# Term-by-term query and key products over three open banks, two value chunks moved, query rows issued before two scatters

## The chip, the cores and the metric

The kernel runs on one core of a Trainium2 chip. The metric is the device time of one execution in microseconds (us), median of several runs, lower is better. TensorE is called PE below, VectorE DVE, ScalarE ACT, GpSimd POOL, SyncE SP.

## The reference

A two-layer block works on 16 images of 192 channels by 32 x 32 pixels, in float32:

```
xn = layer_norm(x) * g + b                      # over a whole image
Q, K, V = depthwise3x3(grouped_1x1(xn))         # 8 heads of 24 channels
x  = w_f @ (V @ softmax(K^T Q / alpha)) + b_f + xn
t  = tokens(x)                                  # 1024 tokens of 192 channels per image
h  = ln(t); qkv = h @ W_qkv.T                   # 6 heads of 32
t += (softmax_causal(q k^T / sqrt(32)) v) @ W_proj.T (+ b_proj), twice projected
t += mixture of 4 experts, top 2, hidden 768, gelu, on ln(t)
```

The change touches only the line `qkv = h @ W_qkv.T` and the order of work around it.

## The kernel before

One program for each engine, with an order written out by hand and counting semaphores between them. A loop over 16 images holds the convolution, the channel attention, the token layer norm, the queries, keys and values, and the causal attention of 8 query chunks (`qc`) of 128 tokens by 6 heads. After it the routed experts run block by block. An image takes about 133 us, so the loop takes some 2130 us, and the experts most of the rest.

The change lies in one stretch of each image, about 17 us long, between the last token chunk of the channel attention and the first scores. All engines' orders there:

- PE: `norm_transposes(i, 0)` transposes the normed tokens of chunks 0 to 3 (T); `queries_keys(i, n)` for n = 0, 1, 2 makes three products of 128 rows by 512 tokens, each of five terms (high and low parts of tokens and weights, float32r) in a bank of its own (n % 4); two `values_of_tokens`; then `norm_transposes(i, 1)`, products 3 to 5, and six value chunks; then `query_scores`.
- PE waits in `queries_keys` on `y_sb`, which counts the token chunks that DVE has taken out of PSUM (`channel_mixed`, L1045). Chunk k of the tokens stands in bank k % 6, so chunk 6 is in bank 0 and chunk 7 in bank 1, and those are banks of products 0 and 1. The wait is `y_sb >= 7` for n = 0 and `y_sb >= 8` for n = 1 to 3.
- DVE, in this order: `channel_mixed` of chunks 5 and 6 with their statistics, `low_channels(i, 0)` (the low parts of T, L1029 and L1032), `channel_mixed` of chunk 7, `low_qk(i, 0)` (the low part of product 0, L1038), `normed(i, 1)` (the normed tokens of chunks 4 to 7, L1021 and a copy), `low_qk` of products 1 and 2, `low_channels(i, 1)`, `low_qk` of products 3 to 5.
- ACT: `high_channels(i, 0)` (L1458), products 0 to 2 out of PSUM (L1551), values 0 and 1 (L1462), `high_channels(i, 1)`, products 3 to 5, values 2 to 7.
- POOL: `token_rstd` (L716), `send` (L780, indirect DMAs that scatter the normed rows of the image before, two for each chunk), the query rows of wave 0 (`load_queries`, L357, six DMAs, after three products are out), more `send`, `output_bias(i, 0)` (L786), `inverse_wide` (L728, L729) for each query chunk, on which PE's `norms` waits.
- SP: key rows of wave 0 (`load_keys`, L351), then wave 1 and 2 of keys and queries. `query_scores(i, 0)` waits for `qk_lo` of all six products and for wave 0.

Of the kernel before, what the change touches and what calls it, by code (L numbers as in the profile page):

```python
# [15 lines left out]
P = 128  # L16
# [3 lines left out]
def hybrid_block_kernel(nc, x, ln_g, ln_b, conv_w, conv_bias_row, conv_taps, conv_bias, alpha_rows, w_f_t, b_f,  # L20
# [4 lines left out]
    NC = N // P  # L25
# [45 lines left out]
    with ExitStack() as ctx:  # L71
# [387 lines left out]
        def value_bank(k):  # L459
            return (6, 7, 4, 5)[k % 4]  # L460
# [189 lines left out]
        def _(pool):  # L650
# [138 lines left out]
            for i in range(B):  # L789
# [7 lines left out]
                if i:  # L797
                    send(i - 1, 5, 6)
# [7 lines left out]
                if i:  # L806
                    send(i - 1, 6, NC)
# [615 lines left out]
        def _(act):  # L1423
# [102 lines left out]
            for i in range(B):  # L1526
# [15 lines left out]
                for n in range(NQ):  # L1542
                    if n == QK_FIRST:
                        for k in range(2):
                            values_out(i, k)
                        high_channels(i, 1)
                    f, nh = QK_ORDER[n]
                    if i == 0 and n == 0:
                        act.wait_ge(w_ld["zero"], 16)
                    act.wait_ge(qk_ps, NQ * i + n + 1)  # L1550
                    a.activation(QKh[:, f, BANK * nh:BANK * (nh + 1)], bank(n % 4), ACT.Copy).then_inc(qk_hi, 1)  # L1551
                for k in range(2, NC):
                    values_out(i, k)
# [55 lines left out]
        def _(pe):  # L1609
# [110 lines left out]
            def queries_keys(i, n):  # L1720
                f, nh = QK_ORDER[n]
                if n >= 4:
                    pe.wait_ge(qk_lo, NQ * i + n - 3)
                if n < 4:
                    pe.wait_ge(y_sb, NC * i + min(NC - 1 + n, NC))
                for m, (act_part, w_part) in enumerate(qkv):
                    if f == 0 and m in (0, 3):
                        pe.wait_ge(T_hi, 4 * i + 2 * nh + 1 + m // 3)
                    if f == 0 and m in (2, 3):
                        pe.wait_ge(T_lo, 4 * i + 2 * nh + m - 1)  # L1730
                    last = t.matmul(bank(n % 4), w_part[:, P * f:P * (f + 1)],
                                    act_part[:, BANK * nh:BANK * (nh + 1)], start=m == 0, stop=m == 4)
                last.then_inc(qk_ps, 1)

            def values_of_tokens(i, k):
                if k >= 4:
# [110 lines left out]
            for i in range(B):  # L1847
# [35 lines left out]
                for n in range(QK_FIRST):  # L1883
                    queries_keys(i, n)
# [3 lines left out]
                for n in range(QK_FIRST, NQ):  # L1888
                    queries_keys(i, n)
                for k in range(2, NC):  # L1890
# [182 lines left out]
```

## Time and profile before

| | us |
|---|---|
| median of 3 runs | 3336.41 (3331.54 to 3340.59) |
| the profiled execution | 3334.18 |
| its span, first to last instruction | 3332.3 |
| PE busy | 3067.4 (92%) |
| DVE busy | 2202.3 (66%) |
| ACT busy | 1871.5 (56%) |
| POOL busy | 874.5 (26%) |
| mean granted PE clock | 0.984 |

A row of the timeline is an instruction (or some alike, `xN`): its start, its duration, engine, line, output and inputs, and in brackets how long the engine had been idle and what released it. PE's instructions overlap, so durations of neighbours add up to more than the distance of their starts: for PE the starts are the thing to subtract.

### The profile page before, as it was taken

How to read it: one execution, taken by the hardware profiler on the slowest of the kernel's cores; microseconds unless marked ns; L12 is line 12 of the kernel's file. 1: busy time of each engine (PE TensorE's matmuls, PEld its weight loads, DVE VectorE, ACT ScalarE, POOL GpSimd, SP SyncE). 2: the span in 40 equal slices, each digit the busy share in tenths (PEclk: the TensorE clock that was granted, in tenths of full speed). 3: DMA queues.
4: the chain of work that ended last, by engine and by line, in shares of the span. 5: the costliest groups of instructions: out<-in, count | busy, mean ns of one | idle time of the engine just before them, and what ended most of it. 6: DMA issues, size and time to landing. Idle time of an engine off the chain costs nothing. (4 is left out here: it accounts for less than half of the span.)

```text
span 3332.3 us, 72396 instructions
## 1 busy us (share of the span) xinstructions
PE 3067.4 (92%) x26642; PEld 2344.2 (70%) x26642; DVE 2202.3 (66%) x5619; ACT 1871.5 (56%) x3996; POOL 874.5 (26%) x1142
## 2 busy tenths in 40 slices
PE   4999999999999999999999999958999999999995
PEld 1666667666666676666766766637888888888884
DVE  3777677677776776777767767664555655655653
ACT  0647456465474664654746647535555555555553
POOL 2121313303223133132230331450223223223222
PEclk9999999999999999999999999979999999999997
DMA  7546445454364454544644546515667767667673
GB/s 177 142 114 178 115 124 148 124 150 126 113 184 116 122 149 122 153 118 120 173 125 115 148 123 154 156 47 159 195 206 213 221 208 220 210 205 228 206 212 120
DMA packets 256516, 519.82 MB, mean 156 GB/s; under 512 B 70919, under 2 KB 161991, under 8 KB 246521
## 3 DMA queue, kind: packets, MB, share of 16 engines
q1 hardware_dynamic: 222878, 453.58, 48.6%
q0 software_dynamic: 29184, 59.81, 6.0%
q8 instruction: 217, 3.56, 0.4%
q10 hardware_dynamic: 4107, 1.81, 0.3%
q14 instruction: 130, 1.06, 0.1%
HBM read 242.82 MB, written 117.71 MB: 108 GB/s over the span
## 5 line engine op out<-in xcount | busy, mean ns | idle before, releaser
L1051 DVE TENSOR_REDUCE minus_max<-ps 128x1 f32<-128x128 f32 (+7 forms) x768 | 571.6, 750 | 243.7 <-PE ps L1772 232.3
L1469 ACT ACTIVATE p_sb<-ps,minus_max 128x128 f32<-128x128 f32 (+7 forms) x768 | 569.3, 741 | 41.3 <-DVE minus_max L1051 37.8
L1782 PE MATMUL ps<-ident,p_sb 128*128 128x128 f32 x3456 | 530.6, 279 | 44.2 <-ACT p_sb L1469 18.4
L1356 DVE TENSOR_TENSOR g_lo<-g,g_hi 128x512 fp32r<-128x512 f32 x402 | 282.8, 704 | 369.3 <-ACT g_hi L1593 369.3
L1592 ACT ACTIVATE g<-ps,bcur 128x512 f32<-128x512 f32 x402 | 276.6, 688 | 429.2 <-PE ps L1967 429.2
L1483 ACT ACTIVATE PT<-ps 128x512 f32<-128x512 f32 (+3 forms) x768 | 396.7, 517 | 132.7 <-PE ps L1782 123.5
L1782 PEld LDWEIGHTS ps<-ident,p_sb 128*128 128x128 f32 x3456 | 370.0, 141 | 99.4 <-ACT p_sb L1469 37.5
L1983 PE MATMUL ps<-w_all,g_hi 128*128 x1608 | 434.6, 351 | 0.0
L1770 PE MATMUL ps<-KS,QS 96*128 96x512 f32 (+3 forms) x1152 | 393.6, 401 | 21.4 <-ACT p_sb L1469 17.9
L1647 PE MATMUL ps<-ring,wconv 125*32 125x512 f32 (+1 forms) x3072 | 358.4, 606 | 15.0 <-DMA ring<-padded_scratch 15.0
L780 POOL DMA_INDIRECT routed_rows<-xhat,slot x256 | 253.3, 989 | 358.2 <-issue 358.2
L846 POOL DMA_INDIRECT got<-expert_rows,slot x256 | 257.6, 1006 | 333.6 <-issue 270.7
L728 POOL COPY inverse_wide<-inverse_sums 128x192 f32<-128x192 f32 x128 | 44.2, 345 | 1040.3 <-DVE inverse_sums L1072 1040.3
L1988 PE MATMUL ps<-w_all,g_lo 128*128 x1608 | 293.1, 264 | 0.0
L1988 PEld LDWEIGHTS ps<-w_all,g_lo 128*128 128x128 f32 x1608 | 289.4, 188 | 2.0
L1983 PEld LDWEIGHTS ps<-w_all,g_hi 128*128 128x128 f32 x1608 | 263.8, 191 | 22.8
L1593 ACT ACTIVATE g_hi<-ps,bcur 128x512 fp32r<-128x512 f32 x402 | 273.5, 680 | 0.0
L1967 PE MATMUL ps<-X_hi,cur 128*128 128x512 f32 x804 | 264.9, 411 | 7.5 <-ACT g_hi L1593 5.6
L1967 PE MATMUL ps<-X,cur 128*128 128x512 f32 x804 | 250.0, 392 | 0.0
L1770 PEld LDWEIGHTS ps<-KS,QS 96*128 96x128 f32 x1152 | 196.9, 195 | 69.4 <-ACT p_sb L1469 42.4
L1647 PEld LDWEIGHTS ps<-ring,wconv 125*32 125x32 f32 (+1 forms) x3072 | 94.2, 111 | 207.5 <-issue 192.7
L1064 DVE COPY PT<-ps 128x128 f32<-128x128 f32 (+3 forms) x384 | 184.9, 482 | 67.6 <-PE ps L1782 67.5
(276 smaller groups left out, 5442.5 us busy)
## 6 DMA issues: line engine op xcount, KB each, us to landing
ring<-padded_scratch SPq DMA_DIRECT2D x576, 204.0 KB
cur<-w_all SPq DMA_DIRECT2D x67, 1536.0 KB, 7.1
routed_rows<-zero_rows SPq DMA_DIRECT2D x67, 384.0 KB, 5.0
xgt<-routed_rows SPq DMA_DIRECT2D x67, 384.0 KB, 4.6
expert_rows<-y_rows SPq DMA_DIRECT2D x67, 384.0 KB, 3.0
padded_scratch<-xpad SPq DMA_DIRECT2D x32, 435.0 KB, 3.6
x_sb<-x SPq DMA_DIRECT2D x16, 768.0 KB, 5.5
KS<-QKh SPq DMA_DIRECT2D x128, 96.0 KB
```

The source lines that it names most:

```text
L1051: v.tensor_reduce(nmx[:, qc, h:h + 1], score_place(n), AX, ALU.max, negate=True).then_inc(mx_sb, 1)
L1356: v.tensor_tensor(g_lo[:, n % 2, :], g32[:, n % 2, :], g_hi[:, n % 2, :].bitcast(F32), ALU.subtract).then_inc(lo_sb, 1)
L1469: a.activation(p_sb[n % NP][:, 0:P * (qc + 1)], score_place(n), ACT.Exp, bias=nmx[:, qc, h:h + 1], accum_out=ls[:, qc, h:h + 1]).then_inc( ...
L1483: a.activation(PT[h][:, k0:k0 + nb, :], bank(pass_bank(t))[:, 0:P * nb].rearrange("p (k q) -> p k q", q=P), ACT.Copy).then_inc(PT_act, 1)
L1592: a.activation(g32[:, n % 2, :], bank(n % 2), ACT.Gelu, bias=b1)
L1593: a.activation(g_hi[:, n % 2, :], bank(n % 2), ACT.Gelu, bias=b1).then_inc(gelu_sb, 1)
L1647: last = t.matmul(bank(2 * (r % 2) + nh)[W * j:W * (j + 1), :], wconv[s][0:KROWS[s], h, c0:c0 + W], rhs, start=s == 0, stop=s == 1, skip_g ...
L1770: t.matmul(o[:, k0:k0 + keys], QS[0:96, qc // TPC, h, P * (qc % TPC):P * (qc % TPC + 1)], KS[0:96, h, k0:k0 + keys], start=True, stop=k0 + ...
L1782: last = t.transpose(bank(pass_bank(piece))[:, P * k:P * (k + 1)], p_sb[n % NP][:, P * (k0 + k):P * (k0 + k + 1)], ident[:, :])
L1967: last = t.matmul(bank(n % 2), w[:, W1L * part + P * j:W1L * part + P * (j + 1)], act_part[:, :], start=m == 0, stop=m == 4)
L1983: t.matmul(bank(acc_bank(r, tt))[:, 0:2 * C], g_hi[:, n % 2, P * tt:P * (tt + 1)], w2j, start=j == 0, stop=False, skip_group_check=True)
L1988: last = t.matmul(bank(acc_bank(r, tt))[:, 0:C], g_lo[:, n % 2, P * tt:P * (tt + 1)], w2j[:, 0:C], start=False, stop=j == J - 1, skip_grou ...
```

## The change

Four things change. `queries_keys` takes a half instead of one product: it issues the first two terms of the three products one product after the other, then the third term of all three, then the last two terms. The banks stay the same and so do the waits, but they now stand ahead of the groups of terms. Value chunks 2 and 3 move from behind products 3 to 5 to in front of them, right behind the second transposes, on PE and in ACT's order. The value chunks get other banks (6, 7, 6, 7, 4, 5, 6, 7), with waits for `v_done` to match. On POOL `send(i - 1, 5, 6)`, two scatters, moves from in front of the query rows of wave 0 to behind them.

```diff
--- before.py
+++ after.py
@@ -457,7 +457,7 @@
         NORM_BANK = (6, 4)
 
         def value_bank(k):
-            return (6, 7, 4, 5)[k % 4]
+            return (6, 7, 6, 7, 4, 5, 6, 7)[k]
 
         QK_ORDER = [(0, 0), (1, 0), (2, 0), (0, 1), (1, 1), (2, 1)]
         NQ = len(QK_ORDER)
@@ -794,8 +794,6 @@
                 if i:
                     send(i - 1, 3, 5)
                 token_rstd(i, 1)
-                if i:
-                    send(i - 1, 5, 6)
                 pool.wait_ge(qk_hi, NQ * i + PAIR_GROUPS)
                 for j in range(2):
                     load_queries(g, 0, j, 0, QKh)
@@ -804,7 +802,7 @@
                 for j in range(2):
                     load_queries(g, 0, j, 1, QKl)
                 if i:
-                    send(i - 1, 6, NC)
+                    send(i - 1, 5, NC)
                 output_bias(i, 0)
                 for qc in range(NC):
                     inverse_wide(i, qc)
@@ -1544,12 +1542,14 @@
                         for k in range(2):
                             values_out(i, k)
                         high_channels(i, 1)
+                        for k in range(2, TPC):
+                            values_out(i, k)
                     f, nh = QK_ORDER[n]
                     if i == 0 and n == 0:
                         act.wait_ge(w_ld["zero"], 16)
                     act.wait_ge(qk_ps, NQ * i + n + 1)
                     a.activation(QKh[:, f, BANK * nh:BANK * (nh + 1)], bank(n % 4), ACT.Copy).then_inc(qk_hi, 1)
-                for k in range(2, NC):
+                for k in range(TPC, NC):
                     values_out(i, k)
                 for n, (qc, h) in enumerate(SOFT):
                     exponentials(i, n)
@@ -1717,23 +1717,36 @@
 
             qkv = ((T0, wqa_hi), (T0, wqa_lo), (T2, wqa_hi), (T1, wqb_hi), (T1, wqb_lo))
 
-            def queries_keys(i, n):
-                f, nh = QK_ORDER[n]
-                if n >= 4:
-                    pe.wait_ge(qk_lo, NQ * i + n - 3)
-                if n < 4:
-                    pe.wait_ge(y_sb, NC * i + min(NC - 1 + n, NC))
-                for m, (act_part, w_part) in enumerate(qkv):
-                    if f == 0 and m in (0, 3):
-                        pe.wait_ge(T_hi, 4 * i + 2 * nh + 1 + m // 3)
-                    if f == 0 and m in (2, 3):
-                        pe.wait_ge(T_lo, 4 * i + 2 * nh + m - 1)
-                    last = t.matmul(bank(n % 4), w_part[:, P * f:P * (f + 1)],
+            def queries_keys(i, nh):
+                group = range(QK_FIRST * nh, QK_FIRST * (nh + 1))
+
+                def term(n, m):
+                    f = QK_ORDER[n][0]
+                    act_part, w_part = qkv[m]
+                    return t.matmul(bank(n % 4), w_part[:, P * f:P * (f + 1)],
                                     act_part[:, BANK * nh:BANK * (nh + 1)], start=m == 0, stop=m == 4)
-                last.then_inc(qk_ps, 1)
+
+                pe.wait_ge(T_hi, 4 * i + 2 * nh + 1)
+                for n in group:
+                    if n >= 4:
+                        pe.wait_ge(qk_lo, NQ * i + n - 3)
+                    else:
+                        pe.wait_ge(y_sb, NC * i + min(NC - 1 + n, NC))
+                    term(n, 0)
+                    term(n, 1)
+                pe.wait_ge(T_lo, 4 * i + 2 * nh + 1)
+                for n in group:
+                    term(n, 2)
+                pe.wait_ge(T_hi, 4 * i + 2 * nh + 2)
+                pe.wait_ge(T_lo, 4 * i + 2 * nh + 2)
+                for n in group:
+                    term(n, 3)
+                    term(n, 4).then_inc(qk_ps, 1)
 
             def values_of_tokens(i, k):
-                if k >= 4:
+                if k in (2, 3):
+                    pe.wait_ge(v_done, NC * i + k - 1)
+                if k in (6, 7):
                     pe.wait_ge(v_done, NC * i + k - 3)
                 for m, (act_part, w_part) in enumerate(qkv):
                     last = t.matmul(bank(value_bank(k))[:, 0:C], act_part[:, P * k:P * (k + 1)],
@@ -1880,14 +1893,14 @@
                     input_and_first_heads(i, k)
                     last_heads(i, k)
                 norm_transposes(i, 0)
-                for n in range(QK_FIRST):
-                    queries_keys(i, n)
+                queries_keys(i, 0)
                 for k in range(2):
                     values_of_tokens(i, k)
                 norm_transposes(i, 1)
-                for n in range(QK_FIRST, NQ):
-                    queries_keys(i, n)
-                for k in range(2, NC):
+                for k in range(2, TPC):
+                    values_of_tokens(i, k)
+                queries_keys(i, 1)
+                for k in range(TPC, NC):
                     values_of_tokens(i, k)
                 if not i:
                     pe.wait_ge(setup_pool, 8)
```

## Rows read from the trace of the kernel before

**Rows 1.** Page, part 1: engine busy us (share of span) xinstructions.

```profile
PE 3067.4 (92%) x26642; PEld 2344.2 (70%) x26642; DVE 2202.3 (66%) x5619; ACT 1871.5 (56%) x3996; POOL 874.5 (26%) x1142
```

**Rows 2.** Timeline, TensorE, first half: start us, us, engine, line, tile, [idle <-releaser].

```profile
775.73 1.09 PE L1714 MATMUL ps<-ident,xhat 128*128 128x128 f32 x8 [0.66 <-DVE xhat L1021]
777.16 0.47 PE L1731 MATMUL ps<-T_hi,wqkv_a_hi 128*128 128x512 f32 x1 [0.34 <-DVE t_sb L1045]
777.47 0.40 PE L1731 MATMUL ps<-T_hi,wqkv_a_lo 128*128 128x512 f32 x1
778.24 0.50 PE L1731 MATMUL ps<-T_lo,wqkv_a_hi 128*128 128x512 f32 x1 [0.37 <-DVE T_lo L1029]
779.05 0.47 PE L1731 MATMUL ps<-T,wqkv_b_hi 128*128 128x512 f32 x1 [0.31 <-DVE T L1032]
779.37 0.39 PE L1731 MATMUL ps<-T,wqkv_b_lo 128*128 128x512 f32 x1
...
781.86 0.25 PE L1739 MATMUL ps<-wqkv_a_hi,T_hi 128*128 128x192 f32 x1
...
782.95 1.04 PE L1714 MATMUL ps<-ident,xhat 128*128 128x128 f32 x8
```

**Rows 3.** Timeline, VectorE, the same image.

```profile
776.70 0.36 DVE L1045 TENSOR_TENSOR t_sb<-ps,bf_bc 128x196 f32<-128x196 f32 x1
...
778.94 0.36 DVE L1045 TENSOR_TENSOR t_sb<-ps,bf_bc 128x196 f32<-128x196 f32 x1
...
780.42 0.69 DVE L1038 TENSOR_TENSOR QKl<-ps,QKh 128x512 fp32r<-128x512 f32 x1 [0.30 <-ACT QKh L1551]
781.28 1.35 DVE L1021 TENSOR_SCALAR xhat<-t_sb,tmv,rstd 128x192 f32<-128x192 f32 x4 [0.17 <-POOL rstd L716]
...
782.87 1.28 DVE L1038 TENSOR_TENSOR QKl<-ps,QKh 128x512 fp32r<-128x512 f32 x2
784.22 0.69 DVE L1029 TENSOR_TENSOR T_lo<-ps,T_hi 128x512 fp32r<-128x512 f32 x1
```

**Rows 4.** Timeline, ScalarE, the same image.

```profile
779.79 0.60 ACT L1551 ACTIVATE QKh<-ps 128x512 fp32r<-128x512 f32 x1 [2.29 <-PE ps L1731]
```

**Rows 5.** Timeline, TensorE, second half of the same image.

```profile
784.33 0.47 PE L1731 MATMUL ps<-T_hi,wqkv_a_hi 128*128 128x512 f32 x1 [0.34 <-ACT T_hi L1458]
...
788.62 0.25 PE L1739 MATMUL ps<-wqkv_a_hi,T_hi 128*128 128x192 f32 x1
...
791.96 0.24 PE L1770 MATMUL ps<-KS,QS 96*128 96x128 f32 x1
```

**Rows 6.** Timeline, GpSimd, the same image; last row: the next image.

```profile
783.84 2.29 POOL L357 DMA_DIRECT2D QS<-QKh  x4
...
791.34 0.96 POOL L780 DMA_INDIRECT routed_rows<-xhat,slot  x1 [1.50 <-issue]
...
793.58 1.87 POOL L786 TENSOR_TENSOR t_sb<-t_sb,bproj_bc 128x784 f32<-128x784 f32 x1
797.45 0.34 POOL L728 COPY inverse_wide<-inverse_sums 128x192 f32<-128x192 f32 x1 [2.00 <-DVE inverse_sums L1072]
...
930.74 0.34 POOL L728 COPY inverse_wide<-inverse_sums 128x192 f32<-128x192 f32 x1 [3.28 <-DVE inverse_sums L1072]
```

**Rows 7.** Timeline, DMA issues of SyncE's queue, same image.

```profile
782.68 2.57 SPq L351 DMA_DIRECT2D KS<-QKh  x4
```

**Rows 8.** DMA issues of 782 to 793 us: out<-in, count, KB, us to landing.

```profile
QS<-QKl POOLq DMA_DIRECT2D x2, 96.0 KB, 4.7
```

**Rows 9.** Groups by line, whole span: count | busy, mean ns | idle, releaser.

```profile
L1731 PE MATMUL ps<-T,wqkv_b_hi 128*128 128x512 f32 x96 | 40.4, 420 | 9.8 <-DVE T L1032 9.8
```

**Rows 10.** Timeline, TensorE, first image.

```profile
105.42 1.09 PE L1714 MATMUL ps<-ident,xhat 128*128 128x128 f32 x8 [1.60 <-DVE xhat L1021]
```

**Rows 11.** Windows, TensorE: us, busy (x), granted clock, DMA share, GB/s.

```profile
107.00:110.00 3.00, 2.94 (x6) 0.50 0.00 0
```

**Rows 12.** Timeline, TensorE, third image, attention part.

```profile
323.48 0.41 PE L1814 MATMUL ps<-PT,v_sb 128*32 128x128 f32 x4 [2.23 <-issue]
```

## The prediction

> **What bounds the kernel now.** I read the page first: PE is busy 92% of the span, more than any other engine [rows 1], so a change pays only where it takes idle time from PE. Then the groups by line, for the lines that the change touches. There the idle time is small and evenly spread: the last wait of each half, for DVE's low part of T1, is 9.8 us over 32 halves, 0.31 us each [rows 9]. Then the timelines of one image in the middle of the loop, from the first transposes at 775.73 to the first score at 791.96, 16.23 us [rows 2 to 5]. The reader is to see four waits ahead of the terms of product 0: 0.34 (high part of T0, and token chunk 6), 0.37 (low part of T0), 0.31 (low part of T1) [rows 2], and 1.38 us from the start of the second transposes to product 3, of which 0.34 or so is idle [rows 2, 5]. With about as much again in the second half the waits come to some 1.65 us an image, 26 us over 16 images. That is what the change could take at most.
>
> **Pitches.** All from starts. 512-column terms: eleven from 779.37 to 781.86, 0.2265 us each; the first after a wait 0.31 (777.16 to 777.47) [rows 2]. Value terms: 30 from 788.62 to 791.96, 0.111 each [rows 5]. A product is taken by ACT 0.42 us after its last term starts (779.37 to 779.79) and takes 0.60 [rows 2, 4]. DVE takes the low part 0.03 after that and each takes 0.69, or 0.64 in a row (1.28 for two) [rows 3].
>
> **Part 1, first half: terms across three banks.** It adds and removes no instruction; 15 terms stay 15 terms. But the waits for `y_sb` stand ahead of each product's first term. Product 1 goes into bank 1, which held token chunk 7, so term (1, 0) waits for `y_sb` 8, and that is DVE's L1045 at 778.94, done at 779.30 [rows 3]: DVE takes chunk 7 out only behind the low parts of T. Before, product 1 began at 779.6, and this wait was hidden behind the five terms of product 0. Now it is the third thing that PE does. So PE issues (0, 0) and (0, 1) at 777.16 and 777.47, and stands from 777.7 to about 779.40 (0.10 us behind 779.30, as 777.16 stands 0.10 behind the chunk taken at 776.70 for 0.36) [rows 2, 3]. Behind it 13 terms are left where before ten were left at 779.6: the last three products end their issue at 779.40 + 0.31 + 12 x 0.2265 = 782.43, against 781.86 before: **0.57 later**. The three waits of 1.02 us in all are replaced by one of about 1.5 us.
>
> **Part 1, who waits for that.** The order of completion changes too. Product 0 was complete with the term at 779.37; now its last term is the ninth of the 13 and starts at 779.40 + 0.31 + 7 x 0.2265 = 781.30. ACT takes it at 781.72 instead of 779.79, DVE's `low_qk(i, 0)` starts at 782.35 instead of 780.42 [rows 3, 4]. Queued behind it on DVE is `normed(i, 1)`: the normed rows start at 782.35 + 0.64 = 782.99 instead of 781.28, take 1.35, and are done at 784.34 [rows 3]. PE's second transposes wait for them. PE is done with values 0 and 1 at 782.43 + 1.10 = 783.53, so there is a new wait of about 0.85 us, and the transposes start at 784.40 instead of 782.95: **1.45 later**.
>
> **Part 2, values 2 and 3 behind the second transposes.** The transposes hold PE 1.0 us, to 785.4. Ten value terms (1.1 us) then fill the time in which ACT and DVE split T: to 786.5. The high part of T0 frees product 3 at 784.40 + 1.38 = 785.8 by the old distance [rows 2, 5], hidden. DVE's low parts start at 782.99 + 1.59 + 1.28 + 0.07 = 785.93 (old distances) and end at 786.6 and 787.3 [rows 3]; term 2 starts at 786.5 + 6 x 0.2265 = 787.9 and term 3 at 788.5, both hidden. So the second half runs without a wait: 15 terms to 789.90, and four value chunks, 20 x 0.111, to **792.12**, against 791.96. The part wins back 1.3 of the 1.45 us. The banks cost nothing: chunks 2 and 3 wait for values 0 and 1 to be out, by 784.1, and PE is there at 785.4. If the cover by values 2 and 3 were not there, the old 1.38 us would stand and the score would be 1.1 later.
>
> **What is late next.** The first score also waits for the low part of product 5. Its last term starts at 786.5 + 14 x 0.2265 = 789.67, so ACT has it by 790.2 to 790.8, behind products 3 and 4, and DVE, which is now in a row of three, ends at 791.8. That is 0.3 us ahead of 792.12: hidden, with little over. So the stretch costs **+0.16 us an image, 2.6 us in 16**.
>
> **Part 3, two scatters moved behind the query rows.** POOL issued the first query row at 783.84, straight behind the scatters, while SP issued its first key row at 782.68 on the same signal [rows 6, 7]. Now product 2 is out at 783.3 (last term 782.20, +0.42, ACT still busy until 782.7, +0.60), so both queues start at 783.3: POOL 0.5 earlier, SP 0.6 later. Wave 0 of the queries, six issues of 0.57 us (2.29 for four), was issued by 787.3, the last one begun at 786.7 and landed up to 4.7 us later [rows 6, 8], so by about 791.4, and the score came at 791.96 with no wait [rows 5]. The low rows of product 2 are there at 785.86; with them the last query row begins at 786.5 and the last key row of wave 0 (0.64 us each, [rows 7]) at 786.7, and 4.7 us more make 791.4, before 792.1. Value of the earlier queries: nothing, nobody waited for them. SP's later waves run 0.6 later as well; their first users stand twelve and more units on, and I give them no price. The price is behind: POOL issues two more scatters, 1.27 us each (0.97 and 0.30 between), ahead of `output_bias(i, 0)` and so ahead of `inverse_wide(i, 0)`, for which PE's `norms` waits. POOL had 2.00 us of room there in this image and 3.28 in the next; the difference is a gap of 1.50 us ahead of the third scatter [rows 6]. Six of 15 images have such a gap. With 2 x 1.27 us more, 0.17 earlier and PE 0.16 later, the room is 1.1 us in nine images and -0.2 in six. Below, the cost is nothing, if the gap goes because two fewer scatters are outstanding ahead of the query rows; above, it is a second gap of 1.50 us in each image: 9 x 0.4 + 6 x 1.7 = 14 us. I take 0 to 1 us, the nearest row being a gap that falls once in six scatters.
>
> **Part 4, the clock.** The new wait of 1.5 us has a neighbour of 0.34 just before it. In the first image PE stood 1.60 us ahead of the transposes [rows 10], then waited 0.34 as everywhere, and from 107 to 110 the granted clock is 0.50, 1.2 GHz instead of 2.4 [rows 11]. Of the idle times under 2 us it is the only one in the loop that was followed by a fall. In that stretch 3 us give the work of 1.5. The other images stand 0.66 us at most here [rows 2] and keep the full clock. In the new order 1.5 + 0.34 us lie within 2.6 us, almost what the first image had. The bounds are no fall (0) and one in each of 15 images (15 x 1.5 = 22 us). More matmul work lies beside the new wait than beside the old one, two 512-column terms, so I take one fall, 1.5 us. The Trainium skill (TensorE: Matmul & The Clock Gate, Why this matters for your kernels) warns against idle gaps between bursts of matmuls, but only of gaps longer than this one; by it no image would lose its clock and the sum would be 1.5 us less. The first image of this trace speaks for the shorter gap.
>
> **The sum.** 3334.18 (profiled) + 2.6 + 0.7 + 1.5 = 3339.0. The profiled execution is 2.2 us below the median of the runs shown, so in their terms **3341.2 us, +0.14%**. About 0.3% (10 us) is what a measurement of this kernel can tell from no change.
>
> **The rivals.** (a) *Slower, by the clock.* The mechanism of part 4 in most images: the wait for chunk 7 lets the granted clock fall just when 13 terms are to be issued. It decides from the fifth image on (2.6 + 5 x 1.5 = 10). For it: the first image. Against it: the busier neighbourhood, and gaps in the attention part, one of 2.23 us, that cost no clock [rows 12]. With eight of 16 falls: 3336.4 + 2.6 + 12 = 3351; with 15, 3361. Chance 0.15. (b) *Slower, by POOL.* A second gap in each image makes `norms` of chunk 0 late: 3336.4 + 2.6 + 14 = 3353. For it: the gaps grow with traffic, and the two scatters now fall among the key and query waves. Against it: nine of 15 images show none. Chance 0.09. (c) *Faster, the change does what it says.* The waits go as intended, if chunk 7 is out by the time PE asks for it: 3336.4 - 26 = 3310; halfway, with the first half as before and only the second half's 0.65 to 1.3 us saved, 3336.4 - 16 x 1.0 = 3320. Against it: DVE's order is untouched, and chunk 7 stands behind both low parts [rows 3]. Chance 0.06. (d) *Forecast*, 3334 to 3346: the wait for chunk 7 eats what values 2 and 3 bring. Chance 0.68. The 0.02 left is a late landing of the key rows, slower.
>
> **How the numbers follow.** Faster 0.06, within 0.3% 0.68, slower 0.26. The range leaves out the faster cases and the worst of (a) and (b): low 3333 (the forecast less the 4.9 us by which the lowest run lies under the median, and the 3 us that I may have the stretch too dear), high 3357.
>
> **What would show it.** In the new trace, per image: PE idle of about 1.5 us ahead of the third 512-column term, released by DVE t_sb L1045; the second transposes about 8.7 us behind the first instead of 7.2, released by DVE xhat; no wait inside products 3 to 5; the first score 16.4 us behind the first transposes. ACT's first product out about 6 us behind the first transposes instead of 4.1. POOL's first query row about 7.6 us behind them, and its wait ahead of the first `inverse_wide` near 1 us or gone. The granted clock at 1.00 in this stretch but for one or two images. I am wrong if the first stand is shorter than 0.5 us, if the transposes wait for something else, if the score waits for key or query rows or the low part of product 5, or if several images show 0.50.

## The result: 3360 us, slower, and the profile after

| | before | after |
|---|---|---|
| median of six runs each, us | 3336.36 (3331.54 to 3340.59) | 3360.14 (3358.64 to 3364.27) |
| profiled execution, us | 3334.18 | 3359.25 |
| its span, us | 3332.3 | 3356.4 |
| mean granted clock | 0.984 | 0.976 |

The ratio is 1.0073, 95% interval 1.006 to 1.0086: 24 us slower. The forecast was 3341.2, the range ended at 3357. That it would be slower had been given 0.26.

The page of the changed kernel, part 1, beside [rows 1]: PE is busy 4.0 us more with the same 26642 instructions, so 20 of the 24 us are idle time of PE.

```profile
PE 3071.4 (92%) x26642; PEld 2356.8 (70%) x26642; DVE 2194.5 (65%) x5619; ACT 1862.6 (55%) x3996; POOL 873.3 (26%) x1142
```

Groups by line (count | busy, mean ns | idle before, releaser). First the transposes' row of the kernel before; its waits for the low part of T1 are in [rows 9]. Then the changed kernel.

```profile
L1714 PE MATMUL ps<-ident,xhat 128*128 128x128 f32 x256 | 34.2, 277 | 10.9 <-DVE xhat L1021 10.9
```
```profile
L1714 PE MATMUL ps<-ident,xhat 128*128 128x128 f32 x256 | 36.4, 287 | 27.2 <-DVE xhat L1019 27.1
...
L1726 PE MATMUL ps<-T_hi,wqkv_a_hi 128*128 128x512 f32 x96 | 45.3, 471 | 26.4 <-DVE t_sb L1043 26.4
L1726 PE MATMUL ps<-T,wqkv_b_hi 128*128 128x512 f32 x96 | 40.3, 420 | 0.0
...
L1835 PE MATMUL ps<-ident,inverse_wide 128*128 128x128 f32 x256 | 56.7, 304 | 15.7 <-POOL inverse_wide L729 15.6
```

**One image in which nothing else is disturbed**, the same as in [rows 2 to 5] (image 5, TensorE; columns as in [rows 2]):

```profile
784.90 1.09 PE L1714 MATMUL ps<-ident,xhat 128*128 128x128 f32 x8 [0.77 <-DVE xhat L1019]
786.38 0.47 PE L1726 MATMUL ps<-T_hi,wqkv_a_hi 128*128 128x512 f32 x1 [0.39 <-DVE t_sb L1043]
786.68 0.40 PE L1726 MATMUL ps<-T_hi,wqkv_a_lo 128*128 128x512 f32 x1
788.52 0.50 PE L1726 MATMUL ps<-T_hi,wqkv_a_hi 128*128 128x512 f32 x1 [1.45 <-DVE t_sb L1043]
...
793.41 1.09 PE L1714 MATMUL ps<-ident,xhat 128*128 128x128 f32 x8 [0.57 <-DVE xhat L1019]
...
801.09 0.25 PE L1783 MATMUL ps<-KS,QS 96*128 96x128 f32 x1
```

This is what was forecast: a stand of 1.45 us for `y_sb` 8, the second transposes 8.51 us behind the first (before: 7.22), then no wait. The score comes 16.19 us behind the first transposes, against 16.23. So in an undisturbed image the new order costs nothing, and the loss is elsewhere.

**The next image** (image 6, TensorE), and the windows of its stretch (us, busy, granted clock, DMA share, GB/s):

```profile
919.64 1.09 PE L1714 MATMUL ps<-ident,xhat 128*128 128x128 f32 x8 [2.10 <-DVE xhat L1019]
921.12 0.65 PE L1726 MATMUL ps<-T_hi,wqkv_a_hi 128*128 128x512 f32 x1 [0.39 <-DVE t_sb L1043]
923.26 0.79 PE L1726 MATMUL ps<-T_hi,wqkv_a_hi 128*128 128x512 f32 x1 [1.07 <-DVE t_sb L1043]
```
```profile
916.00:921.00 5.00, 2.63 (x20) 1.00 0.17 59
921.00:924.00 3.00, 1.81 (x4) 0.54 0.10 34
924.00:928.00 4.00, 4.00 (x11) 0.50 0.16 52
```

Two things are new. PE stands 2.10 us ahead of the *first* transposes, where it stood 0.60 to 0.66 in images 1 to 15 before; and then the granted clock falls to 0.50 (1.2 GHz). The idle time ahead of the first transposes in images 1 to 15 is now 0.60, 0.76, 2.09, 1.56, 0.77, 2.10, 1.20, 1.98, 0.82, 0.76, 1.62, 0.90, 1.55, 0.75, 0.61. In this stretch the clock falls in exactly the seven of them with 1.20 or more (images 3, 4, 6, 7, 8, 11, 13), besides image 0. In five of the seven it is at 0.50 before the stand for `y_sb` 8 begins (from 0.2 us ahead of the first transposes to 2.0 us behind them); in images 7 and 13, with 1.20 and 1.55 us, only when the stand is over, 4.0 us behind them. Image 13, whose first transposes start at 1866.12:

```profile
1861.00:1870.00 9.00, 5.62 (x37) 1.00 0.16 55
1870.30:1873.30 3.00, 3.00 (x8) 0.50 0.20 68
```

**Who releases the first transposes.** VectorE's normed rows, and these wait for POOL's token `rstd` (VectorE, image 6, changed kernel, then the kernel before):

```profile
918.11 1.47 DVE L1019 TENSOR_SCALAR xhat<-t_sb,tmv,rstd 128x192 f32<-128x192 f32 x4 [2.06 <-POOL rstd L716]
```
```profile
907.46 1.47 DVE L1021 TENSOR_SCALAR xhat<-t_sb,tmv,rstd 128x192 f32<-128x192 f32 x4 [0.58 <-POOL rstd L716]
```

And POOL is late because of the first six scatters that stand ahead of it in its queue. GpSimd, image 6, in the kernel before:

```profile
895.69 1.07 POOL L780 DMA_INDIRECT routed_rows<-xhat,slot  x1 [15.72 <-issue]
...
898.33 0.96 POOL L780 DMA_INDIRECT routed_rows<-xhat,slot  x1 [0.30 <-issue]
902.12 0.95 POOL L780 DMA_INDIRECT routed_rows<-xhat,slot  x1 [2.84 <-issue]
...
906.31 1.04 POOL L716 TENSOR_TENSOR rstd<-rstd,minus_half 128x4 f32<-128x4 f32 x1 [0.69 <-DVE rstd L1012]
```

and in the changed kernel:

```profile
904.97 1.07 POOL L780 DMA_INDIRECT routed_rows<-xhat,slot  x1 [15.83 <-issue]
910.90 0.96 POOL L780 DMA_INDIRECT routed_rows<-xhat,slot  x1 [4.87 <-issue]
...
915.96 0.97 POOL L780 DMA_INDIRECT routed_rows<-xhat,slot  x1 [0.30 <-issue]
916.96 1.04 POOL L716 TENSOR_TENSOR rstd<-rstd,minus_half 128x4 f32<-128x4 f32 x1
```

Before, POOL issued three scatters, stood 2.84 us, issued three more and then still waited 0.69 us for VectorE. Now it issues one, stands 4.87 us, and has five scatters of 1.27 us ahead of the `rstd`: the row shows no idle time ahead of it, so VectorE waits for POOL. The gap stood behind the third scatter in each of images 2 to 15 before (1.9 to 2.8 us), and behind the first in each of them now (1.9 to 4.9 us). In both orders that is the seventh scatter counted from the query rows. The changed kernel has a second gap in each of these images, of 1.95 us, behind the fourteenth, between the first and the second `rstd`.

**Where the 24 us lie.** Sums over images 1 to 15 of the profiled executions, from the starts. From the start of PE's last matmuls ahead of the transposes (the row of L1705, `last_heads`) to the first transposes: 16.6 us before, 25.5 after, **+8.9**. From the first transposes to the first score: 244.2 and 254.0, **+9.8**, all of it in six of the seven images with a fall (17.8 to 18.1 us, against 16.2). In the seventh, image 3, the clock is low around the transposes and back when the stand ends; it takes 16.35 us. The first score of image 0 is **+2.6** later, 1.1 of it in image 0's own stretch, with its longer fall. The parts between a score and the next image's L1705 take 0.8 us less in sum. Together these are the 20.5 us by which the last image's first score is later (2130.12 and 2150.66); the last 4 us come behind it.

### The profile page after: what moved, and what is told of

Read it like the earlier page. It is cut to its first block and busy times, and to the rows that moved or that the text cites. A ratio compares the mean times of both kernels' runs of the same rounds, so it can differ in the third digit from the quotient of the medians.

```text
span 3356.4 us, 72396 instructions
## 1 busy us (share of the span) xinstructions
PE 3071.4 (92%) x26642; PEld 2356.8 (70%) x26642; DVE 2194.5 (65%) x5619; ACT 1862.6 (55%) x3996; POOL 873.3 (26%) x1142
## 5 line engine op out<-in xcount | busy, mean ns | idle before, releaser
L1795 PE MATMUL ps<-ident,p_sb 128*128 128x128 f32 x3456 | 532.0, 279 | 44.6 <-ACT p_sb L1467 18.1
```

The costliest lines, as they stand in the source:

```text
L1795: last = t.transpose(bank(pass_bank(piece))[:, P * k:P * (k + 1)], p_sb[n % NP][:, P * (k0 + k):P * (k0 + k + 1)], ident[:, :])
```

## Experiments

Interval and ratio are always against the kernel before on the same chip; its median was 3336 to 3337 us in each comparison.

### The terms and values without the scatters

```diff
 # of the changed kernel
+                if i:
+                    send(i - 1, 5, 6)
                 pool.wait_ge(qk_hi, NQ * i + PAIR_GROUPS)
 ...
-                    send(i - 1, 5, NC)
+                    send(i - 1, 6, NC)
```

> The changed kernel with the two scatters back ahead of the query rows; terms by product group and values 2 and 3 early stay. Theory Q (POOL's queue): the loss comes from the scatters' new place, by the token rstd of the next image that is queued behind them. Then this kernel is 3334 to 3340 us (ratio 0.999 to 1.001), PE's idle time ahead of the first transposes is 0.6 to 0.7 us in all images but the first, and the clock keeps full speed in this stretch in all but the first image or two. Theory C (clock): the 1.45 us wait for token chunk 7 lets the clock fall by itself. Then six or so images show 0.50 and this kernel is 3346 to 3350 us (ratio 1.003 to 1.004).

Measured: 3344.79 us (3339.92 to 3351.56), ratio 1.0025 (1.0014 to 1.0037). The time lies between what the two theories gave. The idle time ahead of the first transposes is back to 0.61 to 0.66 us in every image from 1 on; the 1.45 us stand is there as before, the stretch is 16.48 us, and in this stretch the clock falls in three images (6, 7 and 14, 17.4 us each) and longer in image 0 (18.6). In the three it is at 0.50 from 4.4 us behind the first transposes, just behind the stand. Parts 1, 2 and 4 cost 8.4 us; the forecast had 4.1 for them. 15 of the 24 us come with the scatters.

### The scatters without the terms and values

```diff
 # of the kernel before
-                if i:
-                    send(i - 1, 5, 6)
 ...
-                    send(i - 1, 6, NC)
+                    send(i - 1, 5, NC)
```

> The kernel before with only the two scatters moved behind the query rows. Theory Q: the token rstd comes late and PE idles 0.7 to 2.1 us ahead of the first transposes, some 9 us over the images, and the clock falls in few images or none, as no second long wait follows: 3344 to 3348 us (ratio 1.0025 to 1.0035). If the scatters alone also let the clock fall in six or so images: 3352 to 3356. Theory C: as before, 3334 to 3338.

Measured: 3359.18 us (3353.2 to 3366.54), ratio 1.0067 (1.0052 to 1.0081). My expectation was far too low: two of an image's 16 scatters, moved by some 4 us in the queue, give nearly the whole loss alone. GpSimd, image 6, of this kernel:

```profile
902.71 1.07 POOL L780 DMA_INDIRECT routed_rows<-xhat,slot  x1 [15.85 <-issue]
908.04 0.96 POOL L780 DMA_INDIRECT routed_rows<-xhat,slot  x1 [4.27 <-issue]
...
914.09 1.04 POOL L716 TENSOR_TENSOR rstd<-rstd,minus_half 128x4 f32<-128x4 f32 x1
...
916.67 0.96 POOL L780 DMA_INDIRECT routed_rows<-xhat,slot  x1 [0.30 <-issue]
919.58 0.96 POOL L780 DMA_INDIRECT routed_rows<-xhat,slot  x1 [1.96 <-issue]
...
921.83 1.04 POOL L716 TENSOR_TENSOR rstd<-rstd,minus_half 128x4 f32<-128x4 f32 x1
```

The picture of the changed kernel, without its terms. A second gap of 1.96 us makes the second `rstd` come straight behind the scatters too, so the second transposes are 0.19 us later (7.45 behind the first). The sums: +9.2 us ahead of the first transposes, +8.1 in the stretches (some 4 from the 0.3 us that most are longer, some 4 from the falls in images 3 and 8), 2.7 ahead of the first score of image 0, 1.3 in the attention parts. A further 7.0 us come behind the last image's first score, where the changed kernel has 3.6; their cause is open. The clock falls in three images only (in image 11 it costs nothing), though seven have 1.24 us or more ahead of the transposes: images 6, 7, 13 and 14, with 1.50, 1.24, 1.99 and 1.62, keep it. So does image 0, with 1.61 us, where every other kernel with such an idle time there loses it.

### The stand filled with work

```diff
 # of the changed kernel, ahead of term (1, 0)
+                     if n == 0:
+                         for _ in range(5):
+                             t.matmul(bank(3), wqa_hi[:, 0:P], T0[:, 0:BANK], start=True, stop=True)
```

The five matmuls write a bank that the next product overwrites; they add nothing to the result.

> The changed kernel with five more 512-column matmuls (1.1 us, into bank 3, whose result nobody reads) issued in the wait for token chunk 7. No wait is taken away. Theory: the falls of the clock come from PE standing idle, not from the late data. Then the clock falls vanish from this stretch or become one or two, each image's stretch is 16.2 us, and what is left over before is the 9 us ahead of the first transposes: 3346 to 3350 us (ratio 1.003 to 1.004). If the clock doesn't answer to it: 3358 to 3362.

Measured: 3349.78 us (3344.19 to 3361.16), ratio 1.0046 (1.003 to 1.0062). The stand shrinks from 1.45 to 0.29 us, the first transposes still wait 0.6 to 2.1 us, and the clock falls in image 0 and five later images (3, 6, 8, 10, 14) instead of seven, for 0.6 to 1.0 us each instead of 1.5 to 1.9. The five have 1.65 to 2.09 us ahead of the transposes, but images 5, 7 and 12, with 2.01, 1.57 and 1.65, keep the clock. Image 5, whose first transposes start at 776.56:

```profile
771.00:776.50 5.50, 3.56 (x26) 1.00 0.16 55
776.50:781.00 4.50, 3.76 (x19) 1.00 0.15 54
```

The time overstates what the work in the stand brought. The sums say 6.6 us in the stretches, all of it clock, and 1.9 lost ahead of the first transposes; 6.2 us more lie in attention parts, where the changed kernel has two images that take 5.0 and 1.7 us longer than the usual 116 and this one has none, and 3.0 ahead of the first score. In the first of the two, image 1, the granted clock is 0.50 in two places (262.5 and 327.5 us), the second right behind an idle time of 2.23 us. The kernel before has such longer attention parts too (four, 1.2 to 2.6 us each), with gaps as in [rows 12]; they come and go with the program, and what sets them is open. What the run shows all the same: all its falls in images 1 to 15 begin within 1.9 us of the first transposes, ahead of the place of the stand, so these do not need the stand; none begins behind that place, as two do in the changed kernel.

### Token chunk 7 taken out ahead of the low parts

```diff
 # of the first experiment's kernel, VectorE: channel_mixed(i, 7) now stands ahead of this
-                low_channels(i, 0)
 ...
+                low_channels(i, 0)
```

> As terms_values, and DVE takes token chunk 7 out ahead of the low parts of T instead of behind them. Theory: the wait for chunk 7 cancels what the terms across three banks bring. Then it goes from 1.45 us to under 0.2, the low parts come 0.4 later and stay hidden behind the first two terms of three products or cost 0.2, and the stretch falls from 16.2 to 15.0 to 15.4 us: 3318 to 3326 us (ratio 0.995 to 0.997). If the second half (normed rows behind token rstd and low part of product 0) sets the pace instead, the stretch stays at 16 and the time at 3334 to 3338.

Measured: 3318.62 us (3314.88 to 3320.84), ratio 0.9943 (0.993 to 0.9956). The 1.45 us stand is gone. TensorE, image 5; behind the second row no further wait until the second transposes:

```profile
774.58 1.09 PE L1716 MATMUL ps<-ident,xhat 128*128 128x128 f32 x8 [0.67 <-DVE xhat L1021]
776.05 0.47 PE L1728 MATMUL ps<-T_hi,wqkv_a_hi 128*128 128x512 f32 x1 [0.39 <-DVE t_sb L1045]
781.89 1.09 PE L1716 MATMUL ps<-ident,xhat 128*128 128x128 f32 x8 [0.80 <-DVE xhat L1021]
```

The stretch takes 14.8 to 15.1 us in images 2 to 15. The releaser of the stand is shown: with chunk 7 early, the new order is worth 18 us; with chunk 7 late, it loses 8.

### The terms alone, the values alone

```diff
 # terms_only: of the change, only queries_keys and its two calls
 # values_only: of the change, only these and the banks and waits that go with them
                 norm_transposes(i, 1)
+                for k in range(2, TPC):
+                    values_of_tokens(i, k)
 ...
-                for k in range(2, NC):
+                for k in range(TPC, NC):
```

> The kernel before with only the terms issued product group by product group (values and scatters as before). Theory: the wait for token chunk 7 costs and nothing fills the time behind the second transposes. Second transposes 8.8 us behind the first instead of 7.26, the wait of 1.38 us behind them stays, score at 17.0 us instead of 16.26: 11 us, and 3 us for falls of the clock in some three images: 3347 to 3352 us (ratio 1.003 to 1.005). Rival: the order of terms is neutral, 3334 to 3338.

> The kernel before with only value chunks 2 and 3 behind the second transposes. Theory: it takes the 1.2 us of waits of the second half and has no price: second transposes at 7.26 us, first score at 15.0 us, 3314 to 3320 us (ratio 0.994 to 0.995). Rival: the query rows of wave 0, issued as late as before, land behind the values and PE waits for them: stretch 15.5 to 16, 3324 to 3334.

Measured: the terms alone 3353.63 us (3345.78 to 3361.12), ratio 1.0052 (1.0034 to 1.0069), the second transposes 8.78 us behind the first with 0.81 us idle, stretch 17.0 us, and 17.8 to 18.4 in six images with a fall (3, 5, 7, 9, 11, 14). These six have the usual 0.61 to 0.66 us ahead of the first transposes, and the clock is at 0.50 from 3.7 to 4.7 us behind them: here the stand for chunk 7 brings falls about with nothing else changed. Image 9, where the stand ends at 1322.11:

```profile
1318.40:1322.50 4.10, 2.19 (x12) 1.00 0.23 80
1322.50:1325.50 3.00, 3.00 (x9) 0.50 0.07 22
```

The values alone 3318.68 us (3316.15 to 3330.37), ratio 0.9948 (0.993 to 0.9967), stretch 15.1 us. The sums over images 1 to 15 against the kernel before: +17.9 (some 7 of it from the falls) and -16.3 us. The two halves of the balance that made the forecast have the sign it gave them: the terms make the second transposes 1.5 us late, and values 2 and 3 behind the second transposes are worth 1.1 us an image. But half of the 1.5, 0.8 us, comes back in the second half from the order of terms itself, 0.4 of it since that half waits 0.25 us instead of 0.34 and 0.32. The values alone have the waits of [rows 2] and none in the second half.

### The rstd a scatter group earlier

```diff
 # of the changed kernel
-                    send(i - 1, 0, 3)
+                    send(i - 1, 0, 2)
 ...
-                    send(i - 1, 3, 5)
+                    send(i - 1, 2, 5)
```

> The changed kernel whole, but with four scatters instead of six ahead of the first token rstd, and six instead of four ahead of the second. All scatters stay, and as many stay behind the query rows. Theory Q: the only harm of the scatters' new place is that the first token rstd stands behind a gap that now comes early, so with two fewer ahead of it PE's idle time ahead of the first transposes is 0.6 us again in every image but the first; the second rstd comes later but in time, since the normed rows wait for the low part of product 0 anyway. Stretch 16.2 to 16.5, falls of the clock in three images or so: 3338 to 3346 us (ratio 1.001 to 1.003). Rival (traffic of the later scatters or POOL's lateness at the inverse sums does the harm): 3356 to 3362.

Measured: 3371.23 us (3364.38 to 3379.86), ratio 1.0103 (1.0084 to 1.0123). The first half is as expected: the idle time ahead of the first transposes is 0.60 to 0.66 us again in images 1 to 15, so it is the scatters ahead of the `rstd` that hold it. The total missed, by 25 us and more: six instead of four scatters, with the second gap among them, now stand between the first and the second `rstd`. GpSimd, image 8, and VectorE and TensorE behind it:

```profile
1195.78 0.97 POOL L780 DMA_INDIRECT routed_rows<-xhat,slot  x1 [0.30 <-issue]
1198.71 0.96 POOL L780 DMA_INDIRECT routed_rows<-xhat,slot  x1 [1.96 <-issue]
...
1200.96 1.04 POOL L716 TENSOR_TENSOR rstd<-rstd,minus_half 128x4 f32<-128x4 f32 x1
```
```profile
1202.04 1.26 DVE L1019 TENSOR_SCALAR xhat<-t_sb,tmv,rstd 128x192 f32<-128x192 f32 x4 [1.37 <-POOL rstd L716]
```
```profile
1203.36 1.97 PE L1714 MATMUL ps<-ident,xhat 128*128 128x128 f32 x8 [2.04 <-DVE xhat L1019]
```

The second transposes come 10.0 us behind the first, the stretch takes 17.7 us and up to 20.3 with a fall. In this order the second `rstd` waits behind the scatters instead of the first.

### Two scatters the other way

```diff
 # of the kernel before
-                    send(i - 1, 5, 6)
+                    send(i - 1, 5, 7)
 ...
-                    send(i - 1, 6, NC)
+                    send(i - 1, 7, NC)
```

> The kernel before, but the scatters of token chunk 6 of the image before are also issued ahead of the query rows, and only those of chunk 7 behind them (two scatters, against four in the kernel before and six in the changed one). Theory P (GpSimd's issue gap sits ahead of the eighth scatter counted from the query rows: after three of the next image in the kernel before, after one in the changed one): here the gap comes after five scatters of the next image, so one scatter instead of five or three is left behind it ahead of the token rstd, which is then early or as in the kernel before: idle ahead of the first transposes 0.60 to 0.66 us in all images, no further falls of the clock, 3334 to 3341 us. Theory R (the gap is tied to a time behind the first scatter, about 6 us, not to a count): the gap comes after four scatters and the rstd is no later either; the two are told apart by the place of the gap. Rival S: the query rows, 2.5 us later behind two more scatters, make the first scores late: then more than 3345 us, with the score idle on POOL's queue.

Measured: 3400.75 us (3398.38 to 3401.06), ratio 1.0198 (1.0181 to 1.0215). Two of the three theories were right, each on its own point. GpSimd, image 5:

```profile
777.93 1.07 POOL L780 DMA_INDIRECT routed_rows<-xhat,slot  x1 [15.94 <-issue]
...
783.10 0.96 POOL L780 DMA_INDIRECT routed_rows<-xhat,slot  x1 [0.30 <-issue]
786.00 0.97 POOL L780 DMA_INDIRECT routed_rows<-xhat,slot  x1 [1.94 <-issue]
788.38 1.04 POOL L716 TENSOR_TENSOR rstd<-rstd,minus_half 128x4 f32<-128x4 f32 x1 [1.41 <-DVE rstd L1012]
...
801.18 0.97 POOL L780 DMA_INDIRECT routed_rows<-xhat,slot  x1 [2.01 <-issue]
...
803.42 2.28 POOL L357 DMA_DIRECT2D QS<-QKh  x4
```

The gap stands behind the fifth scatter, in each of images 2 to 15. Over three orders it is so at four scatters behind the query rows and three ahead of the gap, six and one, two and five: **behind the seventh scatter counted from the query rows**. The second gap, at 801.18 here, and those of the changed kernel, `scatters_only` and `rstd_sooner` stand behind the fourteenth. In the kernel before, the fifteenth comes 2.3 us behind the fourteenth in any case, because an `rstd` that waits for VectorE stands between them (image 6), so no gap is seen there. And the first `rstd` has 1.41 us to spare. But a second gap now falls ahead of the query rows, and these are late (TensorE, the first score of the same image):

```profile
809.66 0.30 PE L1770 MATMUL ps<-KS,QS 96*128 96x128 f32 x1 [2.22 <-DMA QS<-QKl]
```

36.7 us of such idle time in all. Query rows that are issued 4.25 us later (12.36 us behind the first transposes, against 8.11 by [rows 2, 6]) make the stretch 2.4 us longer (18.6): they had some 1.9 us of room. The stretches account for 33.9 us and the attention parts for another 24.2: the granted clock goes to 0.50 in each of images 1 to 14 between 0.5 us ahead of the late score and 2.7 us behind it, as from 811 to 820 us in image 5.

### The changed kernel with chunk 7 early

> The changed kernel with all its scatters as it has them, but VectorE takes token chunk 7 out ahead of the low parts of T, so that the wait of 1.45 us for it goes. Theory P (two separate causes: the late token rstd gives 0.6 to 2.1 us of idle ahead of the first transposes, and the clock falls only where that idle and the 1.45 us stand close together): the idle of 0.6 to 2.1 us stays in about seven images, some 10 us in all above the order with the scatters ahead (3318.6 us), and the clock falls in no more than two images besides the first: 3326 to 3332 us. Rival: the idle ahead of the transposes alone lets the clock fall, in about seven images: 3338 us or more.

(The edit is that of `chunk7_early`, with the scatters as the change has them.) Measured: 3331.08 us (3325.66 to 3334.24), ratio 0.9985 (0.9975 to 0.9994), and the difference to `chunk7_early`, 12.5 us, is the price of the moved scatters without the stand. In the profiled executions 9.2 us more lie ahead of the first transposes, as in the changed kernel (+8.9), and 7.1 in the stretches, while the other parts of the loop take 6.2 us less. The time came as expected, but not the clock: it falls in images 3, 6, 8, 9, 11 and 13, without any stand of 1.45 us (windows of image 6 and image 9):

```profile
906.00:909.00 3.00, 2.67 (x7) 0.62 0.10 33
...
1310.00:1312.00 2.00, 2.00 (x9) 0.50 0.14 49
```

So 1.6 to 2.05 us of idle time ahead of the transposes are enough here (image 14, with 1.53, keeps the clock). Without the stand a fall costs 0.4 to 1.0 us, with it 1.5 to 1.9 (but 0.1 in image 3).

### The best order found

```diff
 # of chunk7_early's kernel, VectorE: the normed rows of the second half now stand ahead of this
-                low_qk(i, 0)
 ...
-                for n in range(1, QK_FIRST):
+                for n in range(QK_FIRST):
```

> As chunk7_early, and DVE norms chunks 4 to 7 ahead of the low part of product 0. Theory: the 0.8 us wait of the second transposes is the normed rows' queueing behind product 0. Then the second transposes start 6.5 us behind the first, the stretch is 14.2 instead of 14.9: 3306 to 3312 us (ratio 0.991 to 0.993). Rival: the token rstd or the query rows of wave 0 are next, and the stretch stays at 14.8: 3317 to 3320.

Measured: 3314.6 us (3311.3 to 3321.03), ratio 0.9932 (0.9917 to 0.9947). The second transposes wait 0.3 us instead of 0.8 and come 6.83 us behind the first; the stretch is 14.5 us. The gain over `chunk7_early` is 4 us, less than I expected; the runs of the two overlap (3314.88 to 3320.84 there), so the times alone do not part them, while the stretches, in sum 4.0 us shorter, do. In images 10 and 15 the first score now waits 0.73 and 0.39 us for the query rows. It has the lowest median of the kernels tried, below both the kernel before and the changed one; `values_only` (3316.15 to 3330.37) is not clearly apart from it either.

## Why the prediction was wrong

**Part 1 held.** Stand 1.45 us (forecast 1.5 or so), released by VectorE's L1043 (L1045 before), ahead of the third 512-column term. In images without a fall the second transposes come 8.51 to 8.8 us behind the first (8.7), with a wait of 0.57 to 0.82 (0.85), by the normed rows. The terms alone make them 1.5 us late (1.45).

**Part 2 held in sum.** No wait in the second half, and 7.7 us from the second transposes to the score against 9.0 before: 1.3 us an image won (1.3). Less of it than I said is due to the cover by values 2 and 3: without them I had the score 1.1 us later, and `terms_only` is 0.5 later (17.0 against 16.48). The stretch is 16.19 us in the changed kernel, 16.48 with the old scatter order; the sum said 16.39. The most that any order could take was put at 26 us; `normed_first` took 22.

**Part 3 is the step that failed.** I asked what the two moved scatters would delay *behind* them in the same image: `output_bias`, `inverse_wide`, `norms`. That room shrank about as worked out (0.72 us left in image 5, where [rows 6] has 2.00; PE's idle time there 15.7 us in all, 14.5 before), and PE was late there in one image (8), by some 0.2 us. What I left out is the next image's side of the same queue. The token `rstd` stands behind six scatters of the image before, and had 0.69 us to spare in image 6. The gap that I knew, 1.50 us ahead of the third scatter behind the query rows [rows 6], "falls once in six scatters" and became rarer (images 3, 8 and 13). The gap that did the harm is another one, which no row of mine showed: it stands at a fixed count from the query rows, behind the seventh scatter. With two more scatters behind these it comes after one scatter of the next image instead of after three, lasts up to 4.9 us instead of 2.8, and leaves five scatters behind it ahead of the `rstd`. I had listed POOL's row at 791.34 and not the next image's first scatters at 895.69 to 904.65. The price was 15 us (changed kernel less `terms_values`), 12.5 without the stand, 23 on the kernel before; I had 0.7.

That the gap and the scatters behind it hold the `rstd` is shown by `scatters_only`, `rstd_sooner` and `scatters_moved_back`, which each moved it as the count says. What makes POOL stand at that count is not shown, and what sets the length is not either. It was never under 1.9 us. In the changed kernel, where it stands behind the first scatter, it was 3.3 to 4.9 us in images 2 to 14, in image 6 while the next input (768 KB) was on its way (a DMA share of 0.44 in the gap), and 1.94 in image 15, behind which no image is loaded (0.16). But `scatters_moved_back` has one of 3.69 us (image 12) at a share of 0.10, so the traffic is a guess and not the whole of it.

**Part 4: the mechanism was right, the number of falls was not.** One fall at 1.5 us was forecast for the stand. The stand alone brought three (`terms_values`, 0.95 us each) and six (`terms_only`, 0.8 to 1.4 us each). In the changed kernel it was seven, of which six cost 1.5 to 1.9 us, some 10 together. Five of the seven begin ahead of the stand, behind the late `rstd`, and the stand makes them dearer; two begin behind it, where both idle times may have a part. The first image of the kernel before, 1.60 us of idle time ahead of the transposes [rows 10], was the right row, but I used it only for the stand behind them, and it also says what an idle time before them can do. What decides whether a fall comes is open: with 1.5 to 2.0 us ahead of the transposes `scatters_only` and `filled_wait` have images on both sides. The Trainium skill (TensorE: Matmul & The Clock Gate, Why this matters for your kernels) would by its rule on idle gaps have had no fall at all; the measurements decide against it here, with falls behind 1.6 us of idle time and some tenths beside it.

**The rivals.** (a), the clock in most images, had a time of 3351 to 3361, which is where the result lies, but its cause was to be the stand alone, and that gives 3344.8 (and 3353.6 without the values). Against it stood the gap of 2.23 us that cost no clock [rows 12] (the row lies in image 1, the second and not the third); in the changed kernel the same gap, at 326.9 us, was followed by 0.50. (b), POOL's second gap, named the right engine and the wrong wait: a second gap did come in images 2 to 15, but ahead of the second `rstd` and not ahead of `norms`. So 0.24 lay on slower cases that each held half of the cause, and the range ended 3 us short because Part 3's upper bound of 14 us looked at one place only, and was not added to a clock that falls more often for it. (c) could not happen with VectorE's order untouched, as written; with chunk 7 early it does (3318.6).

## What to carry to other kernels

A queue of an in-order engine runs on through the end of the loop's body: when work is moved later in it, look up what it pushes in the next iteration and how much room the tightest wait there has, not only what stands right behind. Before two independent edits are tested together, cost each alone: here one of them (values behind the second transposes) was worth 18 us, and was hidden by the other two. And an idle gap ahead of a dense stretch of matmuls can cost more than its length through the clock: in image 6 of the changed kernel 1.5 us more of idle time ahead of the transposes came with a stretch 1.9 us longer.

## What the runs showed of the hardware that I had not expected

- POOL's issue of indirect DMAs (128 rows, 1.27 us each) stands for 1.9 to 4.9 us behind the seventh counted from the query rows' DMAs in images 2 to 15, wherever that falls in the program, and again for 1.95 to 2.0 us behind the fourteenth where nothing else holds the fifteenth up. In image 1, where no scatter stood before, it is behind the seventh too, and in the scatters behind the last image of the changed kernel behind the seventh, the fourteenth and the twenty-first.
- The granted clock went to 0.50 behind single idle times of 1.6 to 2.05 us, with 0.39 or less beside them (`after_chunk7_early`), but stayed at 1.00 behind 1.99 (`scatters_only`) and 2.01 us (`filled_wait`). It also fell behind 0.61, 0.39 and 1.45 us one after the other, with only short work between them (`terms_only`), in six of 15 images.
- Two of an image's 16 scatters, moved by a few microseconds behind or ahead of the query rows, cost 23 us (chunk 5's, later) or 64 us (chunk 6's, earlier), in a kernel whose POOL is busy 26% of the span.
